# Weights, context keys and values and router of a decoder layer prepared in the projection stage, and the first rows loaded during attention

## The reference

```python
x = _layernorm(x + _L0_attn_ref(x, Wqkv, Wout, bout))               # causal self-attention over 2048 rows
x = _layernorm(x + _L0_xattn_ref(x, ctx, ctx, mask, Wq, bq, Wk, bk, Wv, bv, Wo, bo))
x = _layernorm(x + _L0_ffn_ref(x, w1, b1, w2, b2, centroids, w_route))
# in the experts: logits = (x/|x|) . (c/|c|) + x . w_route; softmax over the best two of 8;
# h = gelu(x w1[e] + b1[e]); out = sum over e of gate[e] * (h w2[e] + b2[e])
```

## Time and profile before

| | |
|---|---|
| median of 3 runs | 2804.41 us (2798.56 to 2806.45) |
| span of the profiled execution | 2807.5 us, 45159 instructions |
| projection, first to last product | 13.6 to about 265 us |
| attention, until the last store is issued | to 1513.2 us |
| `prepare` | 1516.4 to 1528.2 us |
| slot without experts | 1528.6 to about 1654 us |
| six looped slots, then the last two | 1654 us to the end, about 151 us for a looped slot |

### The profile page before, as it was taken

One profiled execution on the slowest core, in us unless ns is written; L12 is line 12 of the kernel. 1 busy time (PEld: TensorE's weight loads), 2 busy tenths in 40 slices (PEclk: granted clock), 3 DMA queues, 4 the chain that ended last, 5 costly groups with the idle time before them and its releaser, 6 DMA issues. The chain is left out here.

```text
span 2807.5 us, 45159 instructions
## 1 busy us (share of the span) xinstructions
PE 2565.5 (91%) x15124; PEld 1066.4 (38%) x15124; DVE 1922.8 (68%) x3126; ACT 1102.5 (39%) x2002; POOL 782.2 (28%) x275
## 2 busy tenths in 40 slices
PE   8998799998999899999996579999999999999998
PEld 3443233332323223233322335444444545454543
DVE  3333877877788687887863667776767676777765
ACT  3121255554555455555554434232332323232420
POOL 0001144454546163544445211111102021111100
PEclk9999899998999899999998889999999999999999
DMA  4343601102030202020002310101010100001000
GB/s 163 133 146 114 168 9 40 38 22 56 6 72 5 70 9 69 9 69 5 9 8 94 108 44 1 58 1 49 10 43 16 43 17 31 28 1 58 1 16 16
DMA packets 112453, 129.96 MB, mean 46 GB/s; under 512 B 8702, under 2 KB 87294, under 8 KB 112221
## 3 DMA queue, kind: packets, MB, share of 16 engines
q1 hardware_dynamic: 112221, 126.99, 15.1%
HBM read 83.18 MB, written 43.52 MB: 45 GB/s over the span
## 5 line engine op out<-in xcount | busy, mean ns | idle before, releaser
L553 ACT ACTIVATE probs<-st_ps 128x512 f32<-128x512 f32 (+3 forms) x1280 | 628.6, 533 | 597.3 <-PE st_ps L659 303.0
L584 DVE TENSOR_REDUCE seg_max<-s_ps 128x1 f32<-128x512 f32 (+3 forms) x1280 | 700.7, 600 | 232.4 <-PE s_ps L642 138.7
L642 PE MATMUL s_ps<-k_pair,q_pair 96*128 96x512 f16 (+3 forms) x1280 | 442.5, 368 | 69.7 <-DVE seg_max L584 57.2
L659 PE MATMUL st_ps<-q_pair,k_pair 98*128 98x512 f16 (+3 forms) x1280 | 438.6, 363 | 24.0 <-issue 17.8
L462 POOL TENSOR_TENSOR total<-total,probs 128x2048 f32<-128x2048 f32 x88 | 398.2, 4525 | 64.6 <-ACT probs L553 62.0
L679 PE MATMUL o_ps<-probs,v_sb 128*32 128x512 f32 (+3 forms) x2560 | 320.6, 574 | 0.0
L1360 PE MATMUL fps<-x2T,w_p_hi 128*128 128x512 f16 x1024 | 317.3, 379 | 0.0
L1360 PE MATMUL fps<-w_p_hi,hT 128*128 128x512 f16 x1024 | 304.8, 379 | 0.0
L659 PEld LDWEIGHTS st_ps<-q_pair,k_pair 98*128 98x128 f16 x1280 | 118.0, 98 | 375.1 <-ACT probs L553 286.8
L642 PEld LDWEIGHTS s_ps<-k_pair,q_pair 96*128 96x128 f16 x1280 | 126.8, 100 | 275.4 <-DVE seg_max L584 185.5
L462 POOL TENSOR_TENSOR total<-probs 128x2048 f32<-128x2048 f32 x24 | 108.8, 4532 | 356.6 <-ACT probs L553 356.6
(11 more groups left out here) (162 smaller groups left out, 3558.5 us busy)
## 6 DMA issues: line engine op xcount, KB each, us to landing
k_pair<-k_parts SPq DMA_DIRECT2D x96, 128.0 KB, 4.7
q_pair<-q_parts SPq DMA_DIRECT2D x96, 128.0 KB, 5.5
x_raw<-xT_in SPq DMA_DIRECT2D x8, 1024.0 KB, 5.8
q_parts<-qk_out SPq DMA_DIRECT2D x32, 256.0 KB, 2.5
k_parts<-qk_out SPq DMA_DIRECT2D x32, 256.0 KB, 2.5
v_rows<-v_out SPq DMA_DIRECT2D x32, 256.0 KB, 2.0
v_sb<-v_rows SPq DMA_DIRECT2D x8, 1024.0 KB, 10.8
o_parts<-o_out SPq DMA_DIRECT2D x32, 256.0 KB, 2.6
```

The costliest lines, as they stand in the source:

```text
L553: nc.scalar.activation(probs[:, k % NP, h, off:], st_ps[:, p % (2 * NVU) % RING, off:], ACT.Exp, scale=SCALE).then_inc(exp_done.sem, 1)
L584: nc.vector.reduce_max(seg_max[:, h, j, s:s + 1], s_ps[:, slot, 0:width], AX.X).then_inc(s_read.sem, 1)
L642: last = nc.tensor.matmul(s_ps[:, slot, 0:width], q_pair[a][0:NR, h, q0:q0 + P], k_pair[a][0:NR, h, s * CH:s * CH + width], start=True, st ...
L659: last = nc.tensor.matmul(st_ps[:, slot, off:], k_pair[a][:, h, kt * P:(kt + 1) * P], q_pair[a][:, h, c * CH + off:(c + 1) * CH], start=Tr ...
```

## The change

`project_qkv` becomes `project`, written out without a loop over the 8 chunks. Beside the products it also takes what `prepare`, `context` and `apart` did: eleven pieces of weights are loaded, cut by ACT and DVE after products 2 and 6 of a chunk, and either kept in SBUF (`wout`, `wq`, `wo`) or stored to `w_parts` in DRAM (the 8 pieces of `w1` and `w2`). The context's keys and values are made on PE after chunk 4 and stored after chunk 5, the router after chunk 5. `lasting` holds what must survive to the second half. The attention no longer prefetches weights; at the start of its last lap SP waits for the stores of all laps before and loads the first rows. `prepare` is gone, and `chains` starts with the loads of keys, values, mask and then the 16 finished half-precision parts.

```diff
+    SLOTS = [(u, o) for u in range(NC - 1) for o in (2, 6)]
+    PIECE_AT = {SLOTS[n]: n for n in range(NP)}
+    CTX, CENT = 4, 5
...
+            def load_piece(n):
+                src = pieces[n][0]
+                if n >= RAWS:
+                    sp.wait_ge(piece_lo, n - RAWS + 1)
+                sp.dma_start(raw[:, n % RAWS].rearrange("p (a b) -> p a b", a=src.shape[1]), src).then_inc(
+                    raw_loaded[n % RAWS], 16)
+            def store_piece(n):
+                if pieces[n][2] is not None:
+                    sp.wait_ge(piece_lo, n + 1)
+                    sp.dma_start(w_parts[pieces[n][2]], cut[:, n % RAWS]).then_inc(cut_stored[n % RAWS], 16)
...
+                    n = PIECE_AT.get((u, o - 1))
+                    if n is not None:
+                        store_piece(n)
+                        if n + RAWS < NP:
+                            load_piece(n + RAWS)
...
+                if u == 1:
+                    for dst, src in ((raw_k, wk), (raw_v, wv)):
+                        sp.dma_start(dst.rearrange("p (t n) -> p t n", t=KT),
+                                     src.rearrange("(t p) n -> p t n", p=P)).then_inc(kv_raw_loaded, 16)
...
+            def split_piece(n):                       # ScalarE; VectorE makes the low part in the same slot
+                act.wait_ge(raw_loaded[n % RAWS], 16 * (n // RAWS + 1))
...
+                nc.scalar.activation(piece_parts(n)[0], raw[:, n % RAWS], ACT.Copy, scale=WS).then_inc(piece_hi, 1)
...
+                if u == CTX:                          # TensorE
+                    pe.wait_ge(ctx_loaded, 48)
+                    pe.wait_ge(kv_raw_loaded, 32)
+                    for g in range(NG):
+                        bank = product(NUMBER["key", u, g])
+                        for t in range(KT):
+                            last = nc.tensor.matmul(bank[:, 0:KVC], raw_k[:, t * D + g * P:t * D + (g + 1) * P],
+                                                    ctx[:, t], start=(t == 0), stop=(t == KT - 1))
+                        last.then_inc(prod_ready, 1)
...
-                if first is not None and s == TAIL - 1:
-                    for dst, src, loaded in prefetch:
-                        sp.dma_start(dst, src).then_inc(loaded, 16)
+                if end is not None and s == TAIL:
+                    for a in range(2):
+                        sp.wait_ge(o_stored[a], stored_at(CPB * (LAPS - 1)))
+                    load_rows(sp, S, x_rows, o_parts, 0)
...
-def prepare(nc, W, S, x_rows, o_parts, bk, bv, weights, centroids, routeT, bout, bo, bq, b1, b2):
...
-    APART = {"query": 3, "probs0": 2, "out2": 3}
...
             if weights_used:
-                engine.wait_ge(w_lo, len(weights))
+                engine.wait_ge(w_loaded, 16 * len(weights))
...
-            for n, (src, _) in enumerate(weights):
-                if n == len(raws):
-                    sp.wait_ge(keys_done, NG * HG)
...
+            load_context(0)
+            for dst, src in weights:
+                sp.dma_start(dst, src).then_inc(w_loaded, 16)
             load_next(-1, 1)
...
+def lasting(nc, stack):
+    S = {}
+    for name, shape, dt in (("x1", [P, TT, D], F32), ("oT", [P, 2, KT, CH], F16), ("ident", [P, P], F32),
+                            ("power", [P, H], F32), ("bout_bc", [P, D], F32), ("bo_bc", [P, D], F32),
+                            ("bq_sb", [P, KT], F32), ("b1_sb", [P, FT], F32), ("b2_sb", [E, D], F32)):
+        S[name] = stack.enter_context(nc.sbuf_tensor("keep_" + name, shape, dt))
...
```

More of the change, by code:

```diff
@@ L125, in _ @@
                 if n < NU:
[L126 to L130, removed]
-            for u in range(NU):
-                store(LAPS - 1, u)
-            for s in qk_stored:
-                sp.wait_ge(s, stored_at(QL * LAPS))
-            for s in v_stored:
-                sp.wait_ge(s, stored_at(VL * LAPS))
+                    load_x(n)
+            for n in range(RAWS):
+                load_piece(n)
@@ L156, in chunk @@
[L156 to L164 removed]
+                nc.scalar.activation(w_hi[:, :, cols], w_raw[:, :, cols], ACT.Copy, scale=WS).then_inc(w_hi_ready, 1)
@@ new lines, in split_x @@
+            def split_x(u):
+                act.wait_ge(x_loaded[u % NU], 16 * (u // NU + 1))
+                if u >= NU:
+                    act.wait_ge(prod_ready, NUMBER["v", u - NU, PER - 1] + 1)
+                nc.scalar.activation(x_hi[:, u % NU], x_raw[:, u % NU], ACT.Copy, scale=XS).then_inc(x_hi_ready, 1)
+            def split_piece(n):
+                act.wait_ge(raw_loaded[n % RAWS], 16 * (n // RAWS + 1))
+                done = sum(p[2] is not None and k % RAWS == n % RAWS for k, p in enumerate(pieces[:n]))
+                if pieces[n][2] is not None and done:
+                    act.wait_ge(cut_stored[n % RAWS], 16 * done)
+                nc.scalar.activation(piece_parts(n)[0], raw[:, n % RAWS], ACT.Copy, scale=WS).then_inc(piece_hi, 1)
@@ L209, in _, with split_piece @@
+            def split_piece(n):
+                dve.wait_ge(piece_hi, n + 1)
+                hi, lo = piece_parts(n)
+                nc.vector.scalar_tensor_tensor(lo, raw[:, n % RAWS], WS, hi, ALU.mult,
+                                               ALU.subtract).then_inc(piece_lo, 1)
             weights(0)
-            x_lo(0, 0)
+            split_x(0)
             weights(1)
             weights(2)
-            with dve.Fori(0, LAPS - 1) as i:
-                for u in range(NU):
-                    chunk(i, u, False)
@@ L250, in self_attention @@
+def self_attention(nc, S, x_rows, q_parts, k_parts, v_rows, o_parts):
     NR = 3 * DH
@@ L857, in chains @@
     FROM = [sum(FILL[:n]) for n in range(len(FILL))]
-    APART = {"query": 3, "probs0": 2, "out2": 3}
-    assert sum(APART.values()) == len(weights)
     LOOPED = (NC - 2) // 2
@@ L1124, in experts @@
                                          bias=W["b1_sb"][:, n:n + 1], scale=UN).then_inc(gelu_done.sem, 1)
[L1126 to L1139 removed]
+            run(act, program(chain, experts))
         @block.vector
```

527 lines of the change are left out of this document (246 added, 281 removed).

## The result

The changed kernel takes 2788.6 us at the median of five runs (2780.9 to 2791.4), beside 2801.5 for the kernel before on the same chip: 0.9945 of its time, 95% interval 0.9931 to 0.9959, a gain of 11.5 to 19.3 us. The forecast was 2788.5 us. Its profiled execution spans 2786.3 us, where 2791.6 was forecast.

What follows compares the result with a forecast made beforehand. PE was taken to bound the kernel, dense in the projection but often standing between attention and the first looped slot. Gains of 28.0 us less 11.6 and 0.5 net 15.9, so 2804.4 becomes 2788.5 us, range 2780 to 2800.

Steps and rivals of the forecast that it cites:

- A: Entry into `chains`: without `prepare` and the late row loads, "out" starts earlier on PE; gain 13.5 us.
- B: Between "out" and the query: the context's products leave PE, so "turn1" and the query come earlier; gain 4.0 us.
- C: From query to scores: PE no longer waits for keys and mask stored and loaded back; gain 6.6 us.
- D: Scores in the slot: PE runs them at full clock without the wait ahead; gain 1.9 us.
- E: Last two scalings before "probs": POOL runs alone, without DVE's cuts beside it; gain 2.0 us.
- F: Projection: the context's 24 matmuls and the router's transposes land on PE, which has no slack; cost 11.6 us.
- G: Projection's DMAs: 24.4 MB added in chunks 0 to 5, chunk 2 at a share of 0.96; cost 0.
- rival 3: Projection: late transfers in the small rings hold PE, 13 us late, 2796 to 2811 us; chance 0.16.
- Rival 4: Projection: added traffic in chunks 2 and 3 at 175 GB/s or less makes the kernel slower; chance 0.04.
- H: Attention's last lap: row loads issued ahead of the row maxima delay scores; cost 0.5 us, 0 to 1.6 possible.
- Rival 2: Entry of `chains`: a jump that costs 6 us, shrinking the earlier start of "out" by 5.5, to 2794; chance 0.10.
- Rival 5: More on the path than counted, for instance the cuts of "out2": 2780 us or a little less; chance 0.08.

Runs made afterwards that it cites:

- rows_late: The changed kernel, but the first rows are loaded where the chains start, not in attention's last lap; 2797.0 us, 0.9981 of the kernel before.
- before_rows_early: The kernel before with only the first row loads moved into attention's last lap, `prepare` kept; 2800.0 us, 0.9990 of the kernel before.
- in_a_row: The changed kernel with all 24 context products in a row between "out" and "turn1" instead of in the projection; 2778.1 us, 0.9910 of the kernel before.
- the second profiles: Profiles of the kernel before and the changed kernel, both unchanged and run once more; 2799.3 us (one run) and 2786.8 us.
- in_gaps: The changed kernel with the context's products moved from the projection into the slot's holes where PE stood; 2771.6 us, 0.9893 of the kernel before.
- extra1: The changed kernel with one spare 1.05 MB store behind each of the 11 piece loads in the projection; 2791.1 us, 0.9964 of the kernel before.
- the first set of experiments: Follow-up runs timed together: both kernels again unchanged, late row loads, and the context's products done twice; kernel before 2800.9 us, changed kernel 2786.8 us.
- extra2: The changed kernel with two spare stores behind each piece load in the projection, 23 MB more; 2814.7 us, 1.0041 of the kernel before.
- ahead2: The changed kernel with 12 spare 0.52 MB stores between the early row loads and the row maxima; 2802.0 us, 1.0005 of the kernel before.

## Why the prediction was right

**A, 13.5 us: right, 13.6 at PE's start.** "out" starts 3.64 us after the last store instead of 17.23. DVE's last addition gained less, 12.3 us (29.09 to 16.82 behind the store), since PE ran the first 5.4 us of "out" at the lower clock, where before it was 2.7: 13.2 us to the addition instead of 11.9. The prediction had carried the 11.9 over; this is the part of the sum that was mis-sized, and it is why the query starts 24.0 us after "out" and not the 22.6 of its signs. rows_late and before_rows_early show that both parts were needed.

**B, 4.0: 3.8 by the traces,** the query 43.77 us behind the last store before and 27.68 now, 16.1 in sum; 4.1 in in_a_row. **C, 6.6: 6.7**; the scores start at 61.84 and 39.04. **D, 1.9: 2.2**; the fourth block is taken at 66.35 and, in the chain below, at 41.39. **E, 2.0: 2.1**; "probs" starts at 94.67 and 67.65. The three cuts of "out2" gained nothing, as forecast: "probs" to the gate is 45.6 us before and 45.4 after. (POOL's last two scalings took 4.45 us instead of 6.50.) Together 27.2 us of 28.0: the slower "out" takes 1.2, small gains elsewhere give some back. C, D and E are read from the two profiles alone; no run takes them one by one.

The chain of waits of the changed kernel, where these steps follow each other:

```profile
1520.87 13.16 PE cps L1381 x48
...
1544.91 10.53 PE cps L1381 x48
1555.45 0.82 issue
1556.27 2.33 PE cps L1419 x8
1558.62 0.49 DVE soft L1222
```

"out" opens it, then the query, and 0.82 us behind it the scores. No DMA stands in it any more, where the earlier trace rows began with 9.68 us of `oT`.

**F, 11.6: 12.2,** by PE's first product of attention, 274.76 to 286.97 (11.5 between the second profiles), of which 11.8 are the context's products and the router's transposes. It is the one term that worked against the change, it was avoidable, and in_gaps avoided it.

**G, 0: right, and rival 3 is refuted** by the window without a gap. The chance of 0.16 that I gave it was not idle: with another 1 or 2 MB a chunk extra1 has its first gaps. **Rival 4** needed 175 GB/s or less; the chunks ran at 300 and 324.

**H, 0.5: 0, but only just.** SP in attention's last lap:

```profile
1255.66 5.93 SPq L682 DMA_DIRECT2D o_parts<-o_out  x1
1266.36 0.49 SPq L894 DMA_DIRECT2D keep_oT<-o_parts  x1
1266.90 1.24 SPq L659 DMA_DIRECT2D q_pair<-max_rows  x2
```

DMA issues from 1266.3 to 1268.5, with the time from issue to landing, and then the chunk on PE that needs the maxima:

```profile
keep_oT<-o_parts SPq DMA_DIRECT2D x1, 1024.0 KB, 8.1
o_parts<-o_out SPq DMA_DIRECT2D x1, 256.0 KB, 7.3
```

```profile
1276.27 0.39 PE L821 MATMUL st_ps<-q_pair,k_pair 98*128 98x512 f16 x1
```

The wait for the store held the maxima as described, to 11.2 us after the store's issue instead of 5.6. The chunk that needs them began 9.4 us after their issue, and PE did not stand. That is less room than it looks, and less than the "9 us in hand" of my expectations. The maxima have no landing of their own in the profile, but the load of `oT`, issued right ahead of them, landed at 1274.4 (1266.36 + 8.1) and the store issued right behind them at 1275.5 (1268.19 + 7.3). If they landed between the two, as their place in the queue says, they had 1 to 2 us to spare, an estimate. In the second profile `oT` landed at 1271.6 and the chunk began at 1271.92, so there, by the same estimate, it was less than half a microsecond. A cost of 0 is what happened; the 1.6 us at the upper end of the term were close. I: no wait for the weights showed at the first looped slot; the gate's products are followed at once by the next "out".

**Rival 2, the entry as a jump that costs 6 us: refuted,** 3.6 to 3.7 us with the landing of the last store in it, in the eight profiles of the changed kernel and its variants that load the rows early. The Trainium skill, "Runtime: NRT & Kernel Launch", section "Instruction fetch mechanics", has a fetch on a branch out of the fetched pages; if one took place here, it hid behind the landing of the store.

**Rival 5, more on the path than counted:** not in the slot. From the gate to the end the kernel before took 1154.0 and 1156.5 us in its two profiles, the changed one 1156.1 and 1156.2; 1153.9 to 1156.7 is the spread over all profiles.

Three things make the result look better founded than it is. That 2788.5 was forecast and 2788.6 measured is luck: the forecast took 15.9 us off a base of 2804.4, the median of three runs, and with five runs that base is 2801.5 and the gain 12.9, so two errors of 3 us cancelled. The gain by the medians, 12.9 us (14.1 in the first set of experiments), is 1 to 2 less than 27.2 - 12.2 = 15.0, and 2 to 3 less than the forecast; the intervals of the runs can't tell these apart. And the two first profiles, taken alone, would have given 21.2 us, 8.2 of them by the chance of one slow attention.

## What to carry to other kernels

Moving work off a waiting stretch into a dense one is paid at full price on the engine that is the bound: of 27 us gained in the slot the projection took 12 back. Ask first what of the moved work has to leave: here the loads, the cuts and the round trip through DRAM had to go, the products could stay, in the 4 to 12 us in which the same engine stood for the norm and the softmax. Price a moved block by what sticks out of its cover on both sides (4 us of 11 in a row behind "out", nothing in the holes, all of it in the projection), and where two parts cover each other, such as a load and a preparation, expect little from either alone (4.7 and 1.5 us here, of 13.6). Before a difference of spans is explained, profile both kernels twice.

## What the runs showed of the hardware

- The same program's attention took 1221.5 and 1238.5 us in two executions. PE stood for 103.9 and 107.7 us in it; the lower clock was granted for 119.0 and 149.6 us, and 13.2 of the 17.0 us are the same products running slower.
- After standing 10.8 us PE ran "out" at the lower of its two levels (0.5, 1.2 GHz) for 5.4 us; it took 13.16 us, where the query, the same 48 matmuls at full clock, took 10.53. A filled hole kept the clock for the stage behind it ("turn1" 2.03 us in in_gaps against 3.60), but not for the one after that (the query 12.22 us against 10.53).
- Mixed traffic of loads and stores of 0.26 to 1 MB in the projection ran at 336 and 348 GB/s where it held PE (extra2); loads of weight parts alone ran at 408 GB/s in rows_late, from 1532 to 1542 us.
- A 4 KB copy issued behind 8.4 MB in SP's queue was used 13.8 us after its issue (ahead2). The issuing itself is not free either: SP took 9.4 us for twelve copies of 0.5 MB.
- Entering a block cost little beyond the landing of the last store, 2.6 us in the changed kernel's profile: SP issued the next block's first transfer 3.25 us after that store was issued (rows_late), and PE started at 3.64.
